# Feed-forward: activation scales formed inside the quantisation of x, GpSimd's low products after VectorE's high ones, normalisation of x on ScalarE

## What is computed

```python
def fp4_quant_dequant(x):                       # blocks of 16 along the last dim
    scale = jnp.maximum(jnp.max(jnp.abs(xb), axis=-1, keepdims=True) / 6.0, 1e-12)
    xn = xb / scale
    idx = jnp.searchsorted(_MID, jnp.abs(xn))
    q = _GRID[idx] * jnp.sign(xn) * scale
...
def fp4_linear(x, w):
    return jnp.einsum('bsk,nk->bsn', fp4_quant_dequant(x), fp4_quant_dequant(w))
...
h = _layernorm(x, axis=-1) * (1 + cb) + sb
gate = fp4_linear(h, w_gate); y = fp4_linear(h, w_up)
x = x + gb * fp4_linear(jax.nn.silu(gate) * y, w_down)     # 512 -> 1408 -> 512
```

## Time and profile before

| | us |
|---|---|
| three runs: median (lowest to highest) | 4752.75 (4747.89 to 4772.78) |
| profiled execution | 4741.32 |
| its span, first to last instruction | 4739.7 |
| PE busy, share of the span | 3970.0, 84% |
| DVE busy | 3788.9, 80% |
| ACT busy | 1375.0, 29% |
| POOL busy | 1388.1, 29% |

### The profile page before, as it was taken

The page is one execution under the profiler, slowest core; times in us unless marked ns, Lnnn a source line. Parts: engine busy times, 40 slices in busy tenths (PEclk is TensorE's granted clock), DMA queues, the critical chain, the costliest instruction groups (busy, mean ns, idle before and its releaser), DMA issues. The chain is left out here.

```text
span 4739.7 us, 152203 instructions
## 1 busy us (share of the span) xinstructions
PE 3970.0 (84%) x64712; PEld 2691.6 (57%) x64712; DVE 3788.9 (80%) x7929; ACT 1375.0 (29%) x2555; POOL 1388.1 (29%) x735
## 2 busy tenths in 40 slices
PE   4888898888888888888988823699989999899988
PEld 3667676766767676676766712344444444444444
DVE  4677777767777777777777659699999999999997
ACT  2334242333424333342433203212222222222221
POOL 1121212112121111212111115444444444444443
PEclk7899898888988888988889856799999999999999
DMA  3000000000000000000000020001000010100000
GB/s 102 12 30 16 21 25 21 25 17 30 16 22 24 21 25 17 30 16 21 25 17 24 12 88 27 21 27 33 27 32 28 27 33 27 33 27 29 31 27 27
DMA packets 72856, 131.36 MB, mean 28 GB/s; under 512 B 12705, under 2 KB 13473, under 8 KB 72290
## 3 DMA queue, kind: packets, MB, share of 16 engines
q1 hardware_dynamic: 72290, 123.00, 8.0%
HBM read 89.43 MB, written 33.55 MB: 26 GB/s over the span
## 5 line engine op out<-in xcount | busy, mean ns | idle before, releaser
L696 POOL TENSOR_TENSOR xf<-xf,hT 128x1024 f32<-128x1024 f32 x128 | 278.1, 2173 | 1358.7 <-DVE xf L746 1358.7
L862 DVE COPY_PREDICATED Am<-pick,banks 128x64 f32<-128x64 uint8 (+2 forms) x1792 | 460.5, 257 | 125.1 <-DVE Am L862 8.9
L1510 PE MATMUL fbank<-gT,xqT 128*128 128x464 f16 (+1 forms) x2304 | 535.7, 387 | 15.4 <-DVE h L1369 13.1
L1510 PE MATMUL fbank<-uT,xqT 128*128 128x464 f16 (+1 forms) x2304 | 487.9, 362 | 0.0
L1532 PE MATMUL fbank<-dT,hqT 128*128 128x512 f16 x2112 | 477.4, 380 | 0.2 <-ACT hqT L1445 0.2
L707 POOL TENSOR_TENSOR yrs<-yvar,neg_half 128x32 f32<-128x32 f32 x32 | 200.4, 6262 | 827.0 <-DVE yvar L891 827.0
L1510 PEld LDWEIGHTS fbank<-gT,xqT 128*128 128x128 f16 x2304 | 236.7, 104 | 274.5 <-issue 57.1
L1459 ACT ACTIVATE sil<-fbank,und 128x464 f32<-128x464 f32 (+1 forms) x192 | 125.1, 651 | 911.4 <-PE fbank L1510 911.4
L1510 PEld LDWEIGHTS fbank<-uT,xqT 128*128 128x128 f16 x2304 | 225.6, 98 | 231.7 <-issue 1.4
L746 DVE SCALAR_TENSOR_TENSOR xf<-banks,col_maa,sx 128x256 f32<-128x256 f32 x640 | 265.0, 477 | 94.9 <-PE banks L462 94.3
L1326 POOL TENSOR_TENSOR hq<-q16h,s16h 128x1408 f16<-128x1408 f16 x64 | 210.5, 3289 | 440.3 <-DVE s16h L1316 440.3
(11 more groups left out here) (230 smaller groups left out, 8872.3 us busy)
## 6 DMA issues: line engine op xcount, KB each, us to landing
x_tok<-in_L_attn_x SPq DMA_DIRECT2D x32, 512.0 KB, 3.7
xres<-in_L_attn_x SPq DMA_DIRECT2D x32, 512.0 KB, 3.8
x_after_attention<-xres SPq DMA_DIRECT2D x32, 512.0 KB, 3.6
xl<-x_after_attention SPq DMA_DIRECT2D x64, 256.0 KB, 2.7
xr<-x_after_attention SPq DMA_DIRECT2D x64, 256.0 KB, 2.7
out<-xr SPq DMA_DIRECT2D x64, 256.0 KB, 2.0
raw_g<-in_L_wmod SPq DMA_DIRECT2D x3, 1024.0 KB, 5.1
raw_g<-in_L_ffn_w_gate SPq DMA_DIRECT2D x1, 2816.0 KB, 10.7
```

Of the source, the lines that this page charges most:

```text
L696: nc.gpsimd.tensor_tensor(xf[:, j % NXF].rearrange("p g b t -> p (g b) t"), xf[:, j % NXF].rearrange("p g b t -> p (g b) t"), hT[:, :, :, ...
L862: nc.vector.copy_predicated(dst, mask, src).then_inc((done or A_step).sem, 1)
L1510: last = nc.tensor.matmul(GU[2 * pair + t][:, 0:w], xqT[:, u, a, g, :], W[:, b_, g, lo_:hi_], start=(k == 0), stop=(k == 3 * G - 1))
```

## The change

Three edits. In `quantise`, und for x is formed as a step inside the chain, ahead of the subtraction into q, and not behind the high product. `low_part` waits for the high product (`xq_done`, `hq_done`) where it waited for the step ahead of it (`xstep`, `hstep`). The subtract-and-scale of x leaves GpSimd: VectorE forms the negated mean (a new instruction on one element per partition), GpSimd multiplies it by the reciprocal deviation (new, one element per partition), and ScalarE forms hx = x * rstd + nmr with one activation (`act_ln`), which is queued at the end of ScalarE's body behind the copy of xT. The wait for the previous quantisation of x moves with it.

```diff
--- before.py
+++ after.py
@@ -1242,6 +1242,7 @@
         DN = bank[6:8]
         xl = sb("xl", [P, 2, C])
         stats, mv, ve, rstd = sb("statsf", [P, 2, 6]), sb("mvf", [P, 2, 2]), sb("vef", [P, 2]), sb("rstdf", [P, 2])
+        negmu, nmr = sb("negmuf", [P, 2]), sb("nmrf", [P, 2])
         hx, mx = sb("hx", [P, C]), sb("mx", [P, C])
         q16x, q16h = sb("q16x", [P, C], F16), sb("q16h", [P, I_FF], F16)
         sx, ix = sb("sxf", [P, 5, NBX]), sb("ixf", [P, NBX])
@@ -1262,7 +1263,7 @@
         xr_loaded = [sig(f"xr_loaded{u}", 1, 16) for u in range(2)]
         out_stored = [sig(f"out_stored{u}", 1, 16) for u in range(2)]
         st_done, mv_done, ve_done = sig("st_donef", 1), sig("mv_donef", 1), sig("ve_donef", 1)
-        rstd_done = sig("rstd_donef", 1)
+        rstd_done, nmr_done = sig("rstd_donef", 1), sig("nmr_donef", 1)
         ln_done, mod1, mod2 = sig("ln_donef", 1), sig("mod1f", 1), sig("mod2f", 1)
         xstep, hstep = sig("xstep", 16), sig("hstep", 16)
         xq_done, hq_done = sig("xq_done", 1), sig("hq_done", 1)
@@ -1281,7 +1282,7 @@
         def tile_of(j, u):
             return u, bass.ts(j, P)
 
-        def quantise(dve, n, w, src, m, q, s, inv, s16, pw, step, dst, done, freed, q_free):
+        def quantise(dve, n, w, src, m, q, s, inv, s16, pw, step, dst, done, freed, q_free, scales=None):
 
             nb = w // NB
             blocks = lambda ap: ap.rearrange("p (n k) -> p n k", k=NB)
@@ -1307,6 +1308,8 @@
             V.reciprocal(pw[:, 3:4], pw[:, 2:3])
             link(V.tensor_tensor(src, src, m, ALU.add))
             V.tensor_scalar(s[:, 2], s[:, 1], pw[:, 3:4], None, ALU.mult)
+            if scales:
+                scales()
             q_free()
             link(V.tensor_tensor(q[:], src, m, ALU.subtract))
 
@@ -1318,11 +1321,11 @@
             V.tensor_tensor(blocks(dst[:, 0]), blocks(q[:]), bc(s16[:, 0]), ALU.mult).then_inc(done.sem, 1)
             assert k[0] == 11
 
-        def low_part(pool, n, w, q, s16, step, dst, done, freed):
+        def low_part(pool, n, w, q, s16, high, dst, done, freed):
             nb = w // NB
             blocks = lambda ap: ap.rearrange("p (n k) -> p n k", k=NB)
             freed()
-            after(pool, step, n)
+            after(pool, high, n)
             nc.gpsimd.tensor_tensor(blocks(dst[:, 1]), blocks(q[:]), s16[:, 1].unsqueeze(2).to_broadcast([P, nb, NB]), ALU.mult).then_inc(done.sem, 1)
 
         xstep.per = hstep.per = 11
@@ -1353,13 +1356,14 @@
             settled_then(dve, all_max.sem, st_done, n)
             nc.vector.bn_aggr(mv[:, u], stats[:, u]).then_inc(mv_done.sem, 1)
             after(dve, mv_done, n)
+            nc.vector.tensor_scalar(negmu[:, u:u + 1], mv[:, u, 0:1], -1.0, None, ALU.mult)
             nc.vector.tensor_scalar(ve[:, u:u + 1], mv[:, u, 1:2], EPS, None, ALU.add).then_inc(ve_done.sem, 1)
 
         def dve_xq(dve, j, u, n):
             after(dve, mod2, n)
             quantise(dve, n, C, hx[:], mx[:], q16x, sx, ix, s16x, xp[:, u], xstep, xq, xq_done, lambda: after(dve, xT_done, n - 1),
-                     lambda: after(dve, xlow_done, n - 1))
-            nc.vector.tensor_scalar(und[:, u, 0:2], undo[:, 0:2], xp[:, u, 2:3], None, ALU.mult).then_inc(und_done.sem, 1)
+                     lambda: after(dve, xlow_done, n - 1),
+                     lambda: nc.vector.tensor_scalar(und[:, u, 0:2], undo[:, 0:2], xp[:, u, 2:3], None, ALU.mult).then_inc(und_done.sem, 1))
 
         def dve_h(dve, u, n, s):
             lo_, hi_ = W_SLICES[s]
@@ -1403,17 +1407,16 @@
         def pool_x(pool, u, n):
 
             after(pool, ve_done, n)
-            after(pool, xstep, n - 1)
             nc.gpsimd.tensor_tensor(rstd[:, u:u + 1], ve[:, u:u + 1], neg_half[:], ALU.pow).then_inc(rstd_done.sem, 1)
-            settled_then(pool, all_max.sem, rstd_done, n)
-            nc.gpsimd.tensor_scalar(hx[:], xl[:, u], mv[:, u, 0:1], rstd[:, u:u + 1], ALU.subtract, ALU.mult).then_inc(ln_done.sem, 1)
+            after(pool, rstd_done, n)
+            nc.gpsimd.tensor_tensor(nmr[:, u:u + 1], negmu[:, u:u + 1], rstd[:, u:u + 1], ALU.mult).then_inc(nmr_done.sem, 1)
             after(pool, ln_done, n)
             nc.gpsimd.tensor_tensor(hx[:], hx[:], row_cb[:, u], ALU.mult).then_inc(mod1.sem, 1)
             after(pool, mod1, n)
             nc.gpsimd.tensor_tensor(hx[:], hx[:], row_sb[:, u], ALU.add).then_inc(mod2.sem, 1)
 
         def pool_xlow(pool, n):
-            low_part(pool, n, C, q16x, s16x, xstep, xq, xlow_done, lambda: after(pool, xT_done, n - 1))
+            low_part(pool, n, C, q16x, s16x, xq_done, xq, xlow_done, lambda: after(pool, xT_done, n - 1))
 
         def pool_body(pool, j, u, n, do_m, do_out, more):
             if more:
@@ -1421,13 +1424,18 @@
             if two_more(n):
                 pool_x(pool, u, n + 2)
             if do_m:
-                low_part(pool, n, I_FF, q16h, s16h, hstep, hq, hlow_done, lambda: after(pool, hT_done, n - 1))
+                low_part(pool, n, I_FF, q16h, s16h, hq_done, hq, hlow_done, lambda: after(pool, hT_done, n - 1))
             if do_out:
                 v = 1 - u
                 after(pool, xr_loaded[v], j if u else j - 1)
                 after(pool, scaled_out, n - 1)
                 nc.gpsimd.tensor_tensor(xr[:, v], xr[:, v], tmpo[:], ALU.add).then_inc(out_done.sem, 1)
 
+
+        def act_ln(act, u, n):
+            after(act, nmr_done, n)
+            after(act, xstep, n - 1)
+            nc.scalar.activation(hx[:], xl[:, u], ACT.Identity, bias=nmr[:, u:u + 1], scale=rstd[:, u:u + 1]).then_inc(ln_done.sem, 1)
 
         def act_xT(act, u, n):
             after(act, xT_done, n)
@@ -1464,6 +1472,8 @@
                 act_hT(act, n - 1, 1)
             if more:
                 act_xT(act, 1 - u, n + 1)
+            if two_more(n):
+                act_ln(act, u, n + 2)
 
 
         def pe_xT(pe, u, n):
@@ -1585,7 +1595,11 @@
 
             @blk.scalar
             def _(act):
-                run(act, act_body, lambda act: act_xT(act, 0, 0))
+                def first(act):
+                    act_ln(act, 0, 0)
+                    act_xT(act, 0, 0)
+                    act_ln(act, 1, 1)
+                run(act, act_body, first)
 
             @blk.tensor
             def _(pe):
```

## The result

The changed kernel took 4687.97 us (median of four runs, 4683.87 to 4700.36), the kernel before 4754.2 (four runs): ratio 0.9859, 95% interval 0.9825 to 0.9893.

What follows compares the result with a forecast made beforehand. VectorE's fixed chain bounds the feed-forward tile (26.72 us): 23.0 + 0.07 + 1.0 + 2.0 = 26.1, or 25.9 by two tiles' rows, 26.15 with clock falls. Gain 0.57 times 62, taken as 33 us: 4720, range 4692 to 4775.

Steps and rivals of the forecast that it cites:

- high product: VectorE's product writing hq's high part: no longer takes turns with GpSimd's low product, 2.73 to 1.62 us, saving 1.10 a tile.
- und: VectorE's two-element scales, held behind GpSimd's low product of x: moved to where GpSimd is idle, saving 0.86 us a tile.
- the untouched statistics: Next tile's statistics on VectorE, now behind x's high product: not stretched by GpSimd's low product, 0 us, at most 0.86.
- rival 2: Turns come back on the statistics behind x's high product: +0.86 us a tile, 27.0 in all, 4771 us; chance 0.16.
- the negation: Extra one-element instruction on VectorE: adds 0.07 us of issue a tile, at most 0.21.
- x's scale step: VectorE's scale step of x, held by GpSimd's final sum in every tile: 1.0 us a tile in place of 0.36.
- The fall of the clock: TensorE idles 2.0 to 2.5 us before hq's transpositions, so its clock falls, making every second tile slow: 26.4 us.
- the clean tile: A feed-forward tile with TensorE at full clock, where VectorE waits for no SiLU: 25.9 us.
- products on hx: GpSimd's two steps on hx, starting later, take turns with VectorE in h's quantisation: 2.0 us a tile against 1.42.
- SiLU waits: VectorE waits 0.5 us for the third SiLU in every second tile, after TensorE's clock falls.
- Rival 1: Clock holds in every tile, or a step on hx finds more cover: 25.9 or 25.7 us, 4691 to 4702; chance 0.2.
- Rival 3: TensorE starves, its clock falling in every tile: 27.2 us a tile, +30 us, 4783 us; chance 0.16.

Runs made afterwards that it cites:

- e1: Kernel before with only und formed inside the quantisation of x: ratio to before 0.9902, stage 1896.5 us against 1947.9.
- e4: Changed kernel without the move of the normalisation to ScalarE: ratio to before 0.986, stage 1882.9 us against 1893.5 for the changed kernel.
- e5: The changed kernel run again with nothing altered: median 4698.31 us, ratio to before 0.9899, stage 1893.1 us.
- e8: Changed kernel plus six unread products on TensorE ahead of its wait for hq: median 4660.61 us, stage 1878.2 us against 1893.5.
- e14: Changed kernel with GpSimd's final sum one body later and ScalarE's normalisation ahead of its copy of xT: median 4687.12 us, stage 1883.1 us.
- e6: Changed kernel with ScalarE's normalisation queued ahead of the copy of xT: median 4628.88 us, ratio to before 0.9752, stage 1831.2 us.
- e2: Kernel before with only GpSimd's low products waiting for VectorE's high ones: median 4695.39 us, ratio to before 0.9881, stage 1883.4 us.

## Why the prediction was right or wrong

**Right.** The high product (1.10 a tile off VectorE's busy time, though e1 against e4 shows that little of it reaches the stage once und is free), und (0.86 taken, 0.79 measured), the untouched statistics (rival 2 didn't happen), the negation (0.15 busy, 0.07 in the chain), low products of 2.56 always. On the negation: the Trainium skill (SBUF — State Buffer, section Who interferes with whom) lets tensor_scalar contend with GpSimd only when its operands meet the conditions of a mode that takes both ports. That agrees with a trace in which both happen: the one-element negation ran in 0.154 us in the mean, beside GpSimd's low product of x, while the two-element und behind GpSimd's product was held 0.79 in the kernel before. The hold of x's scale step came as worked out in the clean tiles (1.20, that is 1.0), by a margin of 0.11 us where I had 0.1. The fall of the clock came (in 24 of 57 tiles over 3100 to 4600, for every second), with a wait of up to 0.48 for the third SiLU, and so did the clean tile (25.6 to 25.7 for 25.9), and the sign of each edit was right. The larger part of the new waits the prediction didn't have: 0.29 of 0.44 us a tile stand ahead of the second SiLU of the tile after the fall.

**Wrong: two terms of the sum, and one offset.** The forecast's terms were, per tile: high product -1.10, und -0.86, scale step of x +0.64 (0.36 to 1.0), products on hx +0.58, negation +0.07, SiLU waits +0.25, and -0.15 by going from the means (26.1) to the rows of two tiles (25.9): -0.57. The account above has -0.84. The difference of 0.27 is made of these:

1. *The late products on hx, -0.22.* The step "two late ones pay about 1.0 each", 2.0 against 1.42, was sized too high. In a clean tile they hold VectorE 0.89 twice (2.49 - 1.60 and 1.77 - 0.88), in the mean 1.76 in all, and the move cost 0.36 and not 0.58.
2. *One price counted twice, -0.33.* "1.0 per tile" for x's scale step was added in all tiles, and the wait for a SiLU on top in every second one. After a clock fall VectorE comes to the scale step late and most of the sum is over: 0.27 to 0.48 instead of 1.20. The mean hold is 0.65 (0.834 less 0.18), 0.31 more than before and not 0.64 more.
3. Against them: und +0.07, SiLU waits +0.06, and +0.15 because the step to the rows of two tiles took part of the same double counting off already.

Times 64 that is 17 us; the other 4 of the 21 missed are 33 us taken for a sum of 35, and 62 tiles for 64.

4. *The offset.* The last step subtracted the gain from a median of 4752.75, as if the part ahead of the stage cost the same in each kernel. That part ended anywhere within 39 us in 17 executions, and the range had no term for it. With the stage's 54 the forecast would have been 4698, inside the range; the other 12 us of the 66 are put down to the part ahead, by inference. The second set of runs (e5) had the changed kernel at 4698.31, 51 below its own kernel before (4749.12). So on which side of 4692 the median fell was chance; that the stage gained 54 and not 33 was not.

Rival 1 (4691 to 4702, clock holds or the products find cover) was nearest in its time, though the clock does fall; e8 shows it with the clock held. Rival 3, TensorE starving, was unlikely for this kernel but no fancy: e14 comes near it, with a fall in 30 of 59 tiles, and its stage is 52 us above that of e6.

What the prediction missed as an idea: it worked out that the normalisation lands behind the copy of xT and pays for it, and did not see that this is the whole of edit 3's loss, nor that edits 1 and 2 pay for the same 0.79.

## What to carry to other kernels

Where two engines take turns, what an instruction costs is set by what it runs beside: what it is worth to move a step to another engine can hang on its place in that engine's queue, and here the same edit was worth -38 or +30 us by one swap. Count a hold and a wait that end at the same point once, and check two edits that cure the same stall together. Measure a change in the stage it touches, for the code ahead of it can vary by more than the change is worth.

## What the runs showed of the hardware

- **TensorE's clock.** Sixteen transpositions of hq and the twelve gate products behind them, by the idle time just before, over 3100 to 4600 us. At full speed they take 1.05 to 1.07 and 2.51; I call it a fall where either is longer (up to 1.89 and 4.67). In the kernel after: 23 times 1.34 to 1.40 us idle, no fall; 34 times 2.34 to 2.57, 24 falls, of which 6 show in the gate products alone. In e6 none of 53 fell after 1.50 to 1.74. In e14 all 30 fell after 2.94 us or more; in e1 23 of 28 after 3.06 to 3.17, and one after only 1.68 (the gate products took 4.03). So below 2 us a fall was rare, from 2.1 on they are common, and the idle time just before does not decide it alone.
- **A tenth of a microsecond decides a turn.** VectorE's next instruction gets in ahead of GpSimd when GpSimd has to be woken by the instruction before it (e2: und, 0.222 in all 64 tiles), and loses to a GpSimd instruction that follows directly on another (the sum at 3357.61 against the scale step at 3357.72). A small step that loses is held like a wide one: two elements for 0.79 (und, before), 32 columns for 1.02 (x's scale step, after), 88 columns for 0.67 in the mean (h's scale step, e6).
- **The same code ahead of the stage** ended between 2772.6 and 2811.3 us in 17 executions, while the stage behind it repeated within 1 us in three pairs. What varies there I did not look for.
